# An AdaLN transformer block on one core: four half norms turned by transfers and VectorE, and another order at the start

## The reference

```python
mod = (_silu(L0_c) @ L0_wmod).reshape(2, 6, 1, -1)
sa, ca, ga, sb, cb, gb = (mod[:, i] for i in range(6))
# ga, gb: sign kept, magnitude at least 0.25
h = _layernorm(x) * (1 + ca) + sa                 # norm one
Q, K, V = split(h @ c_attn_w + c_attn_b, 3)
base_A = softmax(Q[:, :, :128] @ K[:, :, :128].T * 0.25)        # first pass
cam_ctx = base_A @ V[:, :, :128]
cam_bias = tanh(cam_ctx * cam_gate) @ K[:, :, :128].T * (0.25 * layer_weight)
final_attn = softmax(Q @ K.T * 0.25 + cam_bias)                  # second pass
x = x + ga * ((final_attn @ V) @ c_proj_w + c_proj_b)
h = _layernorm(x) * (1 + cb) + sb                 # norm two
x = x + gb * (gelu(h @ proj1.T + proj1_bias) @ proj2.T + proj2_bias)
```

## Time and profile before

| | us |
|---|---|
| three runs | 308.87, 309.2, 312.12 |
| median | 309.2 |
| the profiled execution | 309.08 |
| its span, first to last instruction | 307.3 |

### The profile page before, as it was taken

The page is one execution under the profiler, slowest core; times in us unless marked ns, Lnnn a source line. Parts: engine busy times, 40 slices in busy tenths (PEclk is TensorE's granted clock), DMA queues, the critical chain, the costliest instruction groups (busy, mean ns, idle before and its releaser), DMA issues.

```text
span 307.3 us, 5121 instructions
## 1 busy us (share of the span) xinstructions
PE 300.9 (98%) x1920; PEld 273.1 (89%) x1920; DVE 223.4 (73%) x439; ACT 158.7 (52%) x268; POOL 107.4 (35%) x131
## 2 busy tenths in 40 slices
PE   7999999999999999999999999999999999999995
PEld 5889989898998988998899888898998999899895
DVE  5776789886899889768733789787789994951631
ACT  2676666553344548708912486645253445941920
POOL 4526734244457548035011132130011344414211
PEclk9999999999999999999999999999999999999999
DMA  7920200736655000010011000004656400001001
GB/s 223 376 87 1 56 15 0 265 79 217 196 192 149 3 0 2 0 53 17 1 36 34 3 0 0 2 0 103 208 170 218 125 2 1 1 2 67 4 17 52
DMA packets 16665, 22.89 MB, mean 74 GB/s; under 512 B 1664, under 2 KB 13696, under 8 KB 16640
## 3 DMA queue, kind: packets, MB, share of 16 engines
q1 hardware_dynamic: 16640, 22.56, 23.1%
HBM read 13.64 MB, written 8.39 MB: 72 GB/s over the span
## 4 chain that ended last, share of the span: by engine, by line
PE 86%; DVE 5%; DMA 2%; ACT 2%; issue 2%; SPq 1%; POOL 1%; DVEq 0%; POOLq 0%
PE a_ps L196 13%; PE a_ps L198 13%; PE a_ps L197 13%; PE s_ps L196 12%; PE s_ps L198 12%; PE s_ps L197 12%; PE t_ps L1230 5%; PE t_ps L1157 2%; DMA wp_raw<-wp 2%; DVE nmax L852 2%; DVE pt_lo L846 1%; ACT prob L603 1%; ACT pt_hi L588 1%; PE a_ps L1139 1%; PE s_ps L1088 1%
## 5 line engine op out<-in xcount | busy, mean ns | idle before, releaser
L603 ACT ACTIVATE prob<-s_ps,nmax 128x1024 f32<-128x1024 f32 x32 | 35.8, 1118 | 48.5 <-DVE nmax L852 48.4
L852 DVE TENSOR_REDUCE nmax<-s_ps 128x1 f32<-128x1024 f32 x32 | 39.0, 1217 | 12.0 <-PE s_ps L198 11.9
L588 ACT ACTIVATE pt_hi<-t_ps 128x512 fp32r<-128x512 f32 x64 | 34.9, 596 | 24.7 <-PE t_ps L1230 20.2
L846 DVE TENSOR_TENSOR pt_lo<-t_ps,pt_hi 128x512 fp32r<-128x512 f32 x64 | 41.1, 683 | 3.8 <-ACT pt_hi L588 3.7
L196 PE MATMUL s_ps<-k_hi,q_hi 128*128 128x512 f32 x96 | 38.2, 398 | 0.0
L198 PE MATMUL s_ps<-k_hi,q_lo 128*128 128x512 f32 x96 | 37.6, 392 | 0.0
L197 PE MATMUL s_ps<-k_lo,q_hi 128*128 128x512 f32 x96 | 37.5, 391 | 0.0
L196 PE MATMUL a_ps<-v_hi,pt_hi 128*128 128x256 f32 x128 | 36.4, 284 | 0.0
L196 PE MATMUL a_ps<-w_hi,pt_hi 128*128 128x256 f32 x128 | 36.4, 284 | 0.0
L197 PE MATMUL a_ps<-w_lo,pt_hi 128*128 128x256 f32 x128 | 36.2, 283 | 0.0
L198 PE MATMUL a_ps<-w_hi,pt_lo 128*128 128x256 f32 x128 | 36.2, 283 | 0.0
(11 more groups left out here) (158 smaller groups left out, 760.6 us busy)
## 6 DMA issues: line engine op xcount, KB each, us to landing
turned<-prob SPq DMA_DIRECT2D x48, 128.0 KB, 2.9
f32s<-turned SPq DMA_DIRECT2D x12, 512.0 KB, 3.6
w_raw<-w_t SPq DMA_DIRECT2D x2, 1024.0 KB, 6.2
out<-x_all SPq DMA_DIRECT2D x16, 128.0 KB, 1.7
x_all<-x SPq DMA_DIRECT2D x4, 256.0 KB, 4.8
wmod_raw<-wmod SPq DMA_DIRECT2D x1, 1024.0 KB, 8.3
x_all<-x SPq DMA_DIRECT2D x2, 512.0 KB, 10.1
wmod_raw<-wmod SPq DMA_DIRECT2D x1, 512.0 KB, 5.1
```

Of the source, the lines that this page charges most:

```text
L588: A(pt_hi[:, (u // 2) % 2, 4 * g:4 * g + 4, (u % 2) * P:(u % 2 + 1) * P], t_bank(b, "p", 2 * u + g)[:, :].rearrange("p (t n) -> p t n", n= ...
L603: A(dst, src, ACT.Exp, bias=nmax[:, u:u + 1], accum_out=rsum[:, u:u + 1]).then_inc(exp_ready, 1)
L846: V.tensor_tensor(pt_lo[dst], t_bank(b, "p", 2 * u + g)[:, :].rearrange("p (t n) -> p t n", n=P), f(pt_hi[dst]), ALU.subtract).then_inc(pt ...
L852: V.tensor_reduce(nmax[:, u:u + 1], s_ps[u % 2][:, :], AX.X, ALU.max, negate=True).then_inc(nmax_ready, 1)
```

## The change

Four norm halves, `(b, n)` = (0, 3), (1, 0), (1, 1) and (1, 3), go the way of the probabilities: `norm_apply` writes `xn` in runs of 32, SP sends and reads it back (`send_norm`), VectorE turns it into `t_ps` (`turn_norm`), and PE's `h_transpose` calls for them are gone. In VectorE's queue `norm_apply(b, 3)` moves from behind n = 3 to behind n = 2, `norm_apply(b + 1, 0)` from behind `ffn_gated(b, 1)` to between `gelu_low(b, 6)` and `gelu_low(b, 7)`, and the turns, `h_split` and `qk_split` calls are placed anew. A `norm_apply` behind a half that travels waits for its writes to have landed, in place of its transposes. In the start: x's first half is loaded in one piece behind the columns, wmod's first part in two, and wqk behind wvt and wp; `modulate_and_transpose` works chunk by chunk of wmod; VectorE takes half of wqk's low part over from GpSimd; `v_project(0, 1)` gets a scores bank of its own; `bias_row` moves from step 2 to before `second_half`, with VectorE's add.

```diff
+DMA_NORMS = ((0, 3), (1, 0), (1, 1), (1, 3))
+TRIPS = ([("p", 0, u) for u in DMA_UNITS] + [("h", 0, 3), ("h", 1, 0), ("h", 1, 1)]
+         + [("p", 1, u) for u in DMA_UNITS] + [("h", 1, 3)])
...
-            prep = {1: [("mod", 1)], 2: [("row", 0)]} if b == 0 else {}
+            prep = {1: [("mod", 1)]} if b == 0 else {}
...
+            A_JOBS += [(b, "v", t) for t in ((0, 1, 2) if b else (0, 2, 3))]
+            A_JOBS += [] if b else [(0, "row", 0), (0, "gate", 0)]
...
+        def v_bank(b, t):
+
+            return s_bank(2) if (b, t) == (0, 1) else a_bank(b, "v", t)
...
+        def sent(*trip):
+
+            return 16 * Q * (TRIPS.index(trip) + 1)
+
+        def back(*trip):
+
+            d, _, n = slot(trip)
+            return d, 16 * n
+
+        def slot(trip):
+
+            d = trip[2] % 2
+            same = [t for t in TRIPS[:TRIPS.index(trip) + 1] if t[2] % 2 == d]
+            return d, same[-2] if len(same) > 1 else None, len(same)
...
-            load_x(0, 0, 2)
             sp.dma_start(cols_sb[:, :], cols).then_inc(cols_in, 16)
-            load_x(1, 2, 2)
-            sp.dma_start(wmod1_raw[:, :, :], wm[:, :, 0:2 * E]).then_inc(wmod1_in, 16)
-            sp.dma_start(wattn_raw[:, :, 0:2 * E], wa[:, :, 0:2 * E]).then_inc(wqk_in, 16)
+            load_x(0, 0, TH)
+            for k in range(EC):
+                sp.dma_start(wmod1_raw[:, k, :], wm[:, k, 0:2 * E]).then_inc(wmod1_in[k], 16)
             sp.dma_start(wvt_raw[:, :, :], wv_t.rearrange("(c p) n -> p c n", p=P)).then_inc(wvt_in, 16)
             sp.dma_start(wp_raw[:, :, :], wp.rearrange("(c p) n -> p c n", p=P)).then_inc(wp_in, 16)
+            sp.dma_start(wattn_raw[:, :, 0:2 * E], wa[:, :, 0:2 * E]).then_inc(wqk_in, 16)
             load_x(2, 4, 2)
...
+            def send_norm(b, n):
+
+                k = TRIPS.index(("h", b, n))
+                wait(sp, xn_ready, b, n + 1)
+                write_rows(k, xn[:, :, :].rearrange("p t e -> p (t e)"))
+                kind, ob, o = slot(TRIPS[k])[1]
+                if kind == "p":
+                    wait(sp, t_psum, ob, 2 * o + 2)
+                else:
+                    wait(sp, ht_psum, ob, 2 * o + 2)
+                read_rows(k)
 
             for b in range(B):
                 for u in DMA_UNITS:
-                    write_probs(b, u)
-                    read_probs(b, u)
+                    send_probs(b, u)
+                send_norm(b, 3)
+                if b + 1 < B:
+                    send_norm(b + 1, 0)
                 for t in range(T):
+                    if t == TH and b + 1 < B:
+                        send_norm(b + 1, 1)
                     wait(sp, y_ready, b, t + 1)
...
-            wqk_low(0)
+            wqk_low(0, (0,))
...
                     inv_std(b + 1, 0)
                 inv_std(b, 3)
+                for t in range(TH):
+                    add_result(pool, G, b, t)
                 if b + 1 < B:
                     inv_std(b + 1, 1)
-                for t in range(TH):
-                    add_result(pool, G, b, t)
                 for t in range(TH, T):
...
+            h_high(1)
             act.wait_ge(wqk_in, 16)
             wqk_high(0)
-            h_high(1)
             h_full(1)
             h_full(0)
-            wqk_high(1)
-            act.wait_ge(wv_in, 16)
-            A(wv_hi[:, :, 0:DK], wattn_raw[:, :, 2 * E:2 * E + DK], ACT.Copy).then_inc(wv_raw_hi, 1)
             act.wait_ge(wvp_psum, 1)
             A(wv_hi[:, :, DK:NV], a_bank(0, "wvp", 0)[:, :].rearrange("p (c n) -> p c n", c=EC), ACT.Copy)\
                 .then_inc(wv_hi_ready, 1)
+            act.wait_ge(wv_in, 16)
+            A(wv_hi[:, :, 0:DK], wattn_raw[:, :, 2 * E:2 * E + DK], ACT.Copy).then_inc(wv_raw_hi, 1)
+            wqk_high(1)
             qk_bias(0, 0)
+            v_high(0, 0)
             qk_high(0)
-            v_high(0, 0)
+            v_high(0, 1)
             qk_bias(0, 1)
-            v_high(0, 1)
+            v_high(0, 2)
             qk_high(1)
-            v_high(0, 2)
             h_high(3)
...
-                if b + 1 < B:
-                    affine(b + 1, 0)
-                    affine(b + 1, 1)
                 for n in range(HC, 2 * HC):
                     gelu(b, n)
+                    if b + 1 < B and n == HC:
+                        affine(b + 1, 0)
+                        affine(b + 1, 1)
                 if b + 1 < B:
+                    qk_bias(b + 1, 0)
                     affine(b + 1, 2)
                     affine(b + 1, 3)
-                    qk_bias(b + 1, 0)
                     A(lw_scr[:, :], lw_arg[:, :], ACT.Exp)
...
+                before = (b, n - 1) if n else (b - 1, 3)
+                if before in DMA_NORMS:
+                    dve.wait_ge(probs_out, sent("h", *before))
+                else:
                     dve.wait_ge(ht_psum, b * 8 + 2 * n)
                 for t in range(TH):
                     j = h * TH + t
-                    last = V.tensor_scalar(xn[:, t, :], x_all[:, b * T + j, :], mv[:, j, 0:1], rstd[:, j:j + 1],
-                                           ALU.subtract, ALU.mult)
+                    o, i = xn[:, t, :], x_all[:, b * T + j, :]
+                    if (b, n) in DMA_NORMS:
+                        o = xn[:, :, :].rearrange("p t e -> p (t e)")\
+                            .rearrange("p (q c t r) -> p t c q r", q=Q, c=EC, t=TH)[:, t, :, :, :]
+                        i = i.rearrange("p (c q r) -> p c q r", c=EC, q=Q)
+                    last = V.tensor_scalar(o, i, mv[:, j, 0:1], rstd[:, j:j + 1], ALU.subtract, ALU.mult)
                 last.then_inc(xn_ready, 1)
...
+            def turn(trip, kind, jobs, signal):
+
+                d, count = back(*trip)
+                dve.wait_ge(probs_back[d], count)
+                for g in range(2):
+                    if (w := read_out(T_JOBS, T_READ_OUT, (trip[1], kind, jobs[g]))) is not None:
+                        dve.wait_ge(*w)
+                    V.transpose(t_bank(trip[1], kind, jobs[g])[:, :].rearrange("p (a i c) -> p i a c", a=TH, i=Q),
+                                quad[:, d, :].rearrange("p (i g a r) -> p g i a r", i=Q, g=2, a=TH)[:, g, :, :, :])\
+                        .then_inc(signal, 1)
...
+            def turn_norm(b, n):
+
+                turn(("h", b, n), "h", (2 * n, 2 * n + 1), ht_psum)
...
+            def wqk_low_dve():
+
+                dve.wait_ge(wqk_hi_ready, 1)
+                src, hi, lo = (a[:, 1, :].rearrange("p (v m n) -> p v m n", m=EC, n=P)[:, :, 0, :]
+                               for a in (wattn_raw[:, :, 0:2 * E], wqk_hi, wqk_lo))
+                V.tensor_tensor(lo, src, f(hi), ALU.subtract).then_inc(wqk_lo_dve, 1)
...
             h_high_dve(0)
+            wqk_low_dve()
             h_low(1)
             h_low(0)
-            pair_stats(1, 0)
             dve.wait_ge(wv_hi_ready, 1)
             V.tensor_tensor(wv_lo[:, :, DK:NV], a_bank(0, "wvp", 0)[:, :].rearrange("p (c n) -> p c n", c=EC),
                             f(wv_hi[:, :, DK:NV]), ALU.subtract).then_inc(wv_lo_ready, 1)
+            pair_stats(1, 0)
             pair_stats(1, 1)
+            v_low(0, 0)
             pair_norm(1, 0)
-            v_low(0, 0)
             pair_norm(1, 1)
             v_low(0, 1)
+            v_low(0, 2)
             h_high_dve(2)
-            v_low(0, 2)
             h_low(3)
             h_low(2)
+            v_low(0, 3)
+            add_bias_row()
             qk_low(0)
             qk_low(1)
-            v_low(0, 3)
             for b in range(B):
...
-                    if n == 3:
+                    if n == 2:
                         norm_apply(b, 3)
+                    if n == HC - 2 and b + 1 < B:
+                        norm_apply(b + 1, 0)
+                ffn_gated(b, 0)
+                ffn_gated(b, 1)
+                turn_norm(b, 3)
+                h_split(b, 6)
+                h_split(b, 7)
+                ffn_gated(b, 2)
+                ffn_gated(b, 3)
                 if b + 1 < B:
                     norm_stats(b + 1, 1)
-                h_split(b, 6)
-                ffn_gated(b, 0)
-                h_split(b, 7)
-                ffn_gated(b, 1)
-                if b + 1 < B:
-                    norm_apply(b + 1, 0)
-                for t in range(2, TH):
-                    ffn_gated(b, t)
-                if b + 1 < B:
-                    h_split(b + 1, 0)
-                    h_split(b + 1, 1)
                 for n in range(HC, 2 * HC):
+                    if n == HC and b + 1 < B:
+                        turn_norm(b + 1, 0)
                     gelu_low(b, n)
-                    if b + 1 < B and n == HC:
+                    if n == HC + 1 and b + 1 < B:
+                        h_split(b + 1, 0)
+                        h_split(b + 1, 1)
+                    if n == HC + 2 and b + 1 < B:
                         norm_apply(b + 1, 1)
                 if b + 1 < B:
+                    qk_split(b + 1, 0)
+                    ffn_gated(b, TH)
```

(40 more changed lines are left out.)

117 lines of the change are left out of this document (56 added, 61 removed).

## The result

The kernel after the change takes 304.63 us (median of 4 runs, 304.42 to 305.25), the kernel before took 309.11 us beside it: the ratio is 0.9853, with a 95% interval from 0.9816 to 0.989. The profiled execution took 304.42 us and has a span of 302.5; before it was 309.08 and 307.3. So 4.66 us went, and the forecast was 4.03.

What follows compares the result with a forecast made beforehand. The prediction took PE's queue, busy 98% of the span, to bound the kernel. From 309.08 us it took 3.03 (blocks 3.48 less stall 0.45) and 1.0 for the start: 305.0 us, range 303.7 to 307.0 at 8 in 10.

Steps and rivals of the forecast that it cites:

- The blocks: Four blocks of eight normalisation transposes leave PE's queue, 0.87 us each, 3.48 us in all.
- The stall: VectorE's norm_apply(1, 0) waits ahead of gelu_low(0, 7) for xn's writes, delaying PE's chunk 7 of ffn_down: 0.45 us lost.
- I take 4.2 + 3.6: Assumed length of a norm's round trip: 4.2 us until the read is issued, 3.6 until it lands, 7.8 us.
- The start: New loading order and value stage before the first scores: 1.0 us gained, from -0.3 to 1.65.
- The loads: New loading order: first projection starts at 11.6 instead of 12.3, gaining 0.7 us, bounds 0 and 1.2.
- a first projection at 12.3 or later: Sign in the profile after that would show rival A.
- rival A: Only the transposes pay, because xn comes later and PE waits for it at the start: 306.1 us, chance 0.13.
- The value stage: v(0, 1) gets its own bank, so v(0, 2) no longer waits: 0.3 us gained, between 0.22 and 0.45, -0.3 at worst.
- bias_row only moves: bias_row goes from step 2 into the value stage, PE doing as many instructions as before; no gain or loss counted.
- B: ScalarE becomes the bound in the FFN stretch and PE waits for gelu_low: 306.8 us, chance 0.09.
- D: Trips take longer than any seen and the second ffn_up waits for h_split in both batches: 307.0 us, chance 0.07.
- C: Late x or wmod lengthens PE's idle gap at the start and its clock drops: 4.9 us slower, 311.0 us, chance 0.04.

Runs made afterwards that it cites:

- run 4: Kernel after with norm (0, 3) written out twice and norm_apply(1, 0) moved behind gelu_low(0, 7): 304.56 us, ratio 0.9857 to the kernel before.
- run 5: The kernel after, unchanged, measured again for its spread: 305.26 us, ratio 0.988 to the kernel before.
- run 7: Kernel after without the scores bank for v(0, 1), value tiles alternating between two banks as before: 305.9 us, ratio 0.9902 to the kernel before.
- run 8: Kernel after with x's first half loaded in two pieces again: 304.95 us, ratio 0.9872 to the kernel before.
- run 10: Kernel after with norm_apply(1, 0) behind gelu_low(0, 7) and x of batch 0 in two loads: 304.51 us, ratio 0.9854 to the kernel before.
- run 12: Kernel after with bias_row and VectorE's add of the row back at step 2: 305.98 us, ratio 0.9894 to the kernel before.
- run 2: Kernel before with the new start alone, the four norm halves staying on PE: 308.35 us, ratio 0.9989 to the kernel before.
- run 9: Kernel after with batch 1's norm two, first half, also sent by transfers: 312.02 us, ratio 1.0101 to the kernel before.
- run 1: Kernel before with the four norm halves sent by transfers and the old start: 306.66 us, ratio 0.9922 to the kernel before.

## Why the prediction was right, point by point

**The blocks, right.** The forecast was 3.48 us in PE; the stretches show 3.53, and 3.54 with the norms alone. "A microsecond taken out of PE's queue should come off the end" held in full, and the second, third and fourth trips cost nothing. The slack of the second ffn_up came out at 1.4 us, the forecast said 0.7 to 1.2; the difference is the shorter write.

**The stall, right in place and wrong in size.** The step that failed is "I take 4.2 + 3.6", the median write of the old trips. Those trips follow close on one another; norm (0, 3) has the queues to itself, and its writes took 3.70 to 3.74 us in all ten profiles in which this norm is written once. The forecast had said "nothing if the writes take 3.7", and that is what came. The price was also above its own terms: with writes of 4.2 they give 0.3 to 0.4 and with 4.45 some 0.55, where the forecast took 0.45 and wrote 0.7. The earlier trace rows had the right case beside the wrong one: the trip from 92.23 to 95.94, 3.71 us, stands alone, the one from 80.40 to 84.85 follows on another. The Trainium skill's "DMA: Bandwidth & Descriptors" (section "Anatomy of one DMA — SWDGE (gpsimd) path"), which the forecast set against the trace, came to no stall as well, but by an estimate of 3.2 us; the row of the lone trip agrees better.

**The start, 1.39 us for 1.0.** The loads were to give 0.7 and gave 1.03 (0.95 at the fold and 0.08 to the first projection). Modulation began at 6.45, as the warm-up ended, and not at 6.8; the fold at 9.37 and not at 9.6. In the other profiles with the new start the fold began at 9.1 to 9.8. PE waited 0.3 to 1.4 us for wmod in six of them (runs 4, 5, 7, 8, 10 and 12) and 0.2 or 0.3 for xn in three (2, 9 and 12). So a single profile gives this gain only to within half a microsecond. One reading in the forecast was off: it has the first projection start at 12.29, which is where the fold's record ends; the projection's own begins at 11.94 before and at 10.91 after. The gain of 0.7 was taken between ends on both sides and stands, but "a first projection at 12.3 or later" could not have shown rival A. The value stage was to give 0.3: it gave 0.26 (0.49 more up to the first scores, with 0.75 of bias_row moved in). The sum was right, but not the reasons. The bank's 0.3 was worked out on the old order of VectorE; in the new order it is worth 1.37 (run 7). And "bias_row only moves" was true against the old kernel (0.75 in, 0.85 out), and wrong as an account of what it does: it takes the place of v(0, 3) as the cover ahead of `second_half`, and 0.77 us go without it (run 12). That these errors came to nearly the right sum is luck.

**The rivals.** A, only the transposes pay: not so, the fold is at 9.37 and PE doesn't wait for xn. Its mechanism exists, at 0.2 to 0.3 us, in runs 2, 9 and 12. B, ScalarE as the bound: no wait of PE for a gelu. Once ScalarE has work queued up behind the two affines, its tiles follow each other every 1.24 us, not the 1.36 of the earlier trace rows. Those 1.36 were PE's pace, an `ffn_up` tile being six matmuls 0.23 us apart, so the forecast had less slack here than there was. Two gelu tiles in a row in the kernel after:

```profile
141.57 0.67 ACT L662 ACTIVATE prob<-s_ps,cols_sb 128x512 f32<-128x512 f32 x1
...
142.81 0.68 ACT L662 ACTIVATE prob<-s_ps,cols_sb 128x512 f32<-128x512 f32 x1
```

D, longer trips: they do occur (5.25 us in run 1) but among the probabilities, not the norms. C, the clock: behind the warm-up it did not fall, as PE had no gap. C read the warm-up's records, 0.43 us apart, as the low level, against a granted clock of 1.00. The other profiles bear that reading out: in run 4 the pace of the same twelve matmuls doubles in their midst. Two windows of its warm-up, one twice as long as the other (stretch, length, busy of PE with the records it touches, granted clock, DMA share, GB/s):

```profile
1.20:3.30 2.10, 2.10 (x5) 1.00 0.45 112
4.30:5.35 1.05, 1.05 (x6) 1.00 1.10 336
```

The starts there are 0.43 us apart up to the eighth record and 0.22 behind it, a factor of two as in run 9 between the levels of 0.50 and 1.00 (0.43 and 0.23). But the granted clock reads 1.00 over both, so for the first microseconds it can't be taken at its word. That the clock is what doubles the pace is argued from this factor; nothing else was tried. When it happens differs from execution to execution: the twelve records fill 4.38 us in runs 4, 10 and 12, 4.9 to 5.0 in 5, 7 and 8, and 5.1 to 5.5 in the other eight. With the new start the six with the short warm-up are the six in which PE waited for wmod.

**The total.** 305.0 was forecast, 304.63 measured, 305.26 in the repeat. Term by term: 3.48 was 3.53, the stall 0.45 was 0, the start 1.0 was 1.39. With the 0.05 of the blocks the errors are all on the same side and make 0.89 us of PE's queue; some 0.2 went back behind its last record, and 304.42, the profiled execution, is 0.6 below the forecast.

## What to carry to other kernels

A transpose by a round trip through memory takes PE's work off the path only where something else stands between the norm and its use. From the end of the applies to the last split it took 12.0 us here for norm (0, 3) and 10.8 for the norm of run 9; where PE came for the result 13.5 us behind the applies the trip was free, where it came 5.0 behind them the kernel got slower than before. Count that distance in the profile first, and time a transfer by a row with the same neighbours in its queue, not by the median. When two edits come together (a reordering and a bank, a removed stage and another in its place), price each in the new order, by taking it out of the finished kernel; the old kernel's waits tell only what the pair is worth.
